# New orders of steps, new signals and new PSUM banks for a gated cross-attention and expert kernel in fp32

## The reference: what is computed

```python
x = x + tanh(g_xattn) * xattn(layernorm(x), ctx, ctx)
x = x + tanh(g_ffn) * ffn(layernorm(x))
```

```python
gate = softmax(h2 @ Wg + bg)
combined = einsum('btd,edf,bte->btf', h2, We, gate)
```

## Time and profile before

| what | value |
|---|---|
| median of 3 runs | 1069.57 us (1068.63 to 1070.08) |
| the profiled execution's own time | 1069.42 us |
| its span | 1067.6 us |
| busy: TensorE, its weight loads | 1012.6 (95%), 831.4 (78%) |
| busy: DVE, ScalarE, GpSimd | 961.4 (90%), 758.7 (71%), 752.5 (70%) |
| chain that ended last | TensorE 87%, DVE 5%, GpSimd 4% |

### The profile page before, as it was taken

One profiled execution on the slowest core, in us unless ns is written; L12 is line 12 of the kernel. 1 busy time (PEld: TensorE's weight loads), 2 busy tenths in 40 slices (PEclk: granted clock), 3 DMA queues, 4 the chain that ended last, 5 costly groups with the idle time before them and its releaser, 6 DMA issues.

```text
span 1067.6 us, 32201 instructions
## 1 busy us (share of the span) xinstructions
PE 1012.6 (95%) x12870; PEld 831.4 (78%) x12870; DVE 961.4 (90%) x2176; ACT 758.7 (71%) x1564; POOL 752.5 (70%) x1111
## 2 busy tenths in 40 slices
PE   1568999999999999999999999999999999999998
PEld 0447788788888888888888888888888888888787
DVE  7778888999999999999999999999999999998996
ACT  6678877776677777668777666877766687776541
POOL 4578877787677778767778766777876677787531
PEclk9989999999999999999999999999999999999999
DMA  9501000011000001100100100010111000000000
GB/s 311 169 21 31 12 24 29 31 31 31 23 28 25 22 31 31 32 21 24 29 22 32 32 31 22 21 32 21 32 32 31 22 22 31 22 21 12 12 11 30
DMA packets 38915, 38.67 MB, mean 36 GB/s; under 512 B 3440, under 2 KB 38512, under 8 KB 38768
## 3 DMA queue, kind: packets, MB, share of 16 engines
q1 hardware_dynamic: 38384, 36.59, 10.9%
q0 software_dynamic: 384, 0.04, 0.0%
HBM read 28.23 MB, written 8.39 MB: 34 GB/s over the span
## 4 chain that ended last, share of the span: by engine, by line
PE 87%; DVE 5%; POOL 4%; issue 1%; ACT 1%; DMA 0%; SPq 0%; POOLq 0%; DVEq 0%; ACTq 0%
PE ps L2302 15%; PE ps L2304 14%; PE ps L2303 14%; PE ps L2333 10%; PE ps L2348 9%; PE ps L2341 5%; PE ps L2317 5%; PE ps L2382 3%; PE ps L2373 3%; PE ps L2296 2%; PE ps L2358 2%; DVE hk L1770 2%; PE ps L2366 1%; PE ps L2367 1%; PE ps L2325 1%
## 5 line engine op out<-in xcount | busy, mean ns | idle before, releaser
L1434 DVE SCALAR_TENSOR_TENSOR z<-ps,gate,z 128x256 f32<-128x256 f32 x512 | 238.5, 472 | 37.9 <-PE ps L2304 29.0
L2302 PE MATMUL ps<-we_hi,h_hi 128*128 128x512 f32 (+2 forms) x640 | 240.5, 376 | 0.6 <-DVE z L1434 0.4
L2304 PE MATMUL ps<-we_hi,h_lo 128*128 128x512 f32 (+2 forms) x640 | 224.1, 350 | 0.0
L2303 PE MATMUL ps<-we_lo,h_hi 128*128 128x512 f32 (+2 forms) x640 | 223.7, 349 | 0.0
L2302 PEld LDWEIGHTS ps<-we_hi,h_hi 128*128 128x128 f32 x640 | 120.4, 188 | 36.7 <-issue 12.6
L2333 PE MATMUL ps<-qf,kf 64*128 64x256 f32 x1024 | 129.2, 391 | 9.1 <-POOL kf L549 4.5
L2304 PEld LDWEIGHTS ps<-we_hi,h_lo 128*128 128x128 f32 x640 | 120.2, 188 | 17.1
L2303 PEld LDWEIGHTS ps<-we_lo,h_hi 128*128 128x128 f32 x640 | 120.8, 189 | 11.5
L2333 PEld LDWEIGHTS ps<-qf,kf 64*128 64x128 f32 x1024 | 96.4, 191 | 29.8 <-issue 11.3
L2348 PE MATMUL ps<-att,v 128*32 128x256 f32 (+1 forms) x2048 | 109.0, 329 | 3.1 <-POOL att L540 0.9
L911 ACT ACTIVATE att<-ps 128x512 f32<-128x512 f32 x32 | 19.1, 597 | 116.8 <-PE ps L2333 116.7
(11 more groups left out here) (232 smaller groups left out, 3079.7 us busy)
## 6 DMA issues: line engine op xcount, KB each, us to landing
x_in<-in_x SPq DMA_DIRECT2D x32, 256.0 KB, 2.6
c_in<-in_ctx SPq DMA_DIRECT2D x32, 256.0 KB, 2.6
out<-z SPq DMA_DIRECT2D x32, 256.0 KB, 2.2
c_chunk<-in_ctx SPq DMA_DIRECT2D x14, 512.0 KB, 8.0
stage<-in_L_ffn_We SPq DMA_DIRECT2D x2, 1024.0 KB, 10.0
c_chunk<-in_ctx SPq DMA_DIRECT2D x2, 256.0 KB, 6.5
stage_b<-in_L_ffn_bup SPq DMA_DIRECT2D x1, 256.0 KB, 6.9
stage_q<-in_L_ffn_Wq SPq DMA_DIRECT2D x1, 256.0 KB, 6.4
```

The lines of the kernel that those rows point to most:

```text
L1434: return dve.scalar_tensor_tensor(out=z[b % 2][:, t, :], in0=ps[:, bank, offset:offset + D], scalar=gate[:, t, ex:ex + 1], in1=z[b % 2][:, ...
L2302: pe.matmul(out, a_hi(c), b_hi(c), start=(c == 0), stop=False)
L2303: pe.matmul(out, a_hi(c), b_lo(c), start=False, stop=False)
L2304: last = pe.matmul(out, a_lo(c), b_hi(c), start=False, stop=(c == C - 1))
```

## The change

Nothing is computed in another way. On all five engines the first slots, the steady slot and the last steps are listed in a new order; the steady loop starts at n = 5 in place of 6. The waits follow the new order, the signals are grouped anew (13 semaphores for TensorE's steps in the loop, 12 before), and 43 of the 48 entries of `BANK` are new. TensorE's slot, as the lists read (`+1` stands for batch n + 1):

```diff
-h2_t1(-3) h2_t0(-3) mm13(-4) dn(-1) fq(+1) mm1g(-3) mm0g(-3) o_tr(-2) mm12(-3) kv0(-1) kv1(-1) o(-2)
-mm10(-3) mm11(-3) X00(+1) X01(+1) Y0(+1) Y1(+1) X11(+1) X10(+1) av0(+1) s(-1) av1(+1)
-mm00(-3) mm01(-3) hn_t(0) mm02(-3) fkp(+2) av2(+1) pv(-1) av3(+1) fk(+2) mm03(-3) nt_t(+1) qq(0)
+o(-2) mm0g(-3) mm1g(-3) dn(-1) fq(+1) mm00(-3) mm11(-3) mm10(-3) kv1(-1) kv0(-1) mm01(-3)
+X01(+1) X00(+1) Y0(+1) X11(+1) X10(+1) Y1(+1) av0(+1) s(-1) av1(+1) hn_t(0)
+mm12(-3) mm13(-3) mm02(-3) mm03(-3) av2(+1) pv(-1) av3(+1) fkp(+2) fk(+2) nt_t(+1)
+o_tr(-1) h2_t0(-2) h2_t1(-2) qq(0)
```

GpSimd's slot:

```diff
-pq0(+1) pk0(+1) d_v(-1) pq2(+1) pq3(+1) v1(+1) pq1(+1) z0(-2) x1(0) v_bd(-1) m01(+1) m00(+1) k_lo(+2)
-g_r(0) yb(-1) m10(+1) q_r(+2) r2(-2) m11(+1) pk2(+2) q_lo(+2) pk1(+2) o_n(-1) pk3(+2)
+pk1(+1) q_lo(+1) z0(-2) x1(0) pk2(+1) pq2(+1) pq0(+1) d_v(-1) pq1(+1) pk0(+1) pk3(+1) pq3(+1) g_r(0)
+r2(-2) m00(+1) k_lo(+2) m01(+1) q_r(+2) m10(+1) v_bd(-1) m11(+1) yb(-1) o_n(-1) v1(+2)
```

The part of the diff with the banks and with the waits of the steps that the prediction speaks of:

```diff
-BANK = dict(stab=0, fk0=6, fk1=4, fk2=3, fk3=7, fq0=0, fq1=2, fq2=4, fq3=1, x000=3, x001=1, x010=0, x011=5,
-            y00=3, y01=7, av0=3, x100=0, x101=2, x110=5, x111=4, y10=1, y11=6, av1=2, nd0=2, nd1=0, ht=1,
+BANK = dict(stab=2, fk0=2, fk1=3, fk2=5, fk3=4, fq0=6, fq1=7, fq2=2, fq3=0, x000=6, x001=4, x010=1, x011=7,
+            y00=2, y01=1, av0=2, x100=3, x101=0, x110=7, x111=5, y10=4, y11=6, av1=7, nd0=1, nd1=0, ht=3,
...
+            def X01_(b):
+                if b >= 4:
+                    pe.wait_ge(*at("a00", b - 4))
+                if b >= 2:
+                    pe.wait_ge(*at("bqq", b - 2))
...
+                pe.wait_ge(*at("pq3", b))
+                first_keys(b, 0, 1, BANK["x010"], BANK["x011"]).then_inc(*up("X01", b))
...
             def Y0_(b):
...
+                pe.wait_ge(*at("x010", b))
+                second_keys(b, 0, BANK["y00"], BANK["y01"]).then_inc(*up("Y0", b))
```

More of the change, by code:

```diff
@@ L386, in _ @@
             load_x_(6)
-            store_(1)
-            load_x_(7)
-            load_c_(8)
-            for n in range(6, NB + -1):
+            for n in range(5, NB + -1):
                 slot(n)
@@ new lines, in g_r_ @@
+            @per_batch
+            def g_r_(b):
+                pool.wait_ge(*at("g_bn", b))
+                if b >= 1:
+                    pool.wait_ge(*at("y", b - 1))
+                for which in range(2):
+                    pool.tensor_scalar(shift_f[:, which, :], mvg[:, :, 0], -1.0, 1.0, ALU.mult, ALU.mult)
+                pool.tensor_tensor(r_f[:, :, :].rearrange("p a b -> p (a b)"), var_f[:, :, :].rearrange("p a b -> p (a b)"),
+                                   neg_half[:, 0:2 * T], ALU.pow).then_inc(*up("r_f", b))
+                pool.wait_ge(*at("r_f", b))
+                pool.tensor_tensor(shift_f[:, :, :], shift_f[:, :, :], r_f[:, :, :], ALU.mult).then_inc(*up("g_r", b))
@@ L1994, in _ @@
+            h_lo_(1)
+            h_tr_(1)
+            wo_hi_()
+            q_bn_(1)
+            y00_(0)
+            h_lo_(2)
+            y01_(0)
+            x_t_(1)
+            y10_(0)
+            we_lo2_()
+            y11_(0)
+            c_t_(2)
+            b_kv_()
+            wo_lo_()
+            wdn_hi_()
+            we_lo3_()
             h_tr_(2)
-            wo_hi_()
+            off_tok_()
+            wq_hi_()
             den_(0)
             o_x_(0)
-            wq_hi_()
+            we_lo1_()
@@ L2492, in o_, with mm00_ @@
-            @per_batch
-            def o_(b):
-                if not b:
-                    pe.wait_ge(*at("bqq", b + 1))
-                if b >= 4 and b + 3 < NB:
-                    pe.wait_ge(*at("eq3", b + 3))
-                pe.wait_ge(*at("ot_lo", b))
-                for t in range(T):
-                    last = three_passes(ps[:, BANK["o"], t * D:(t + 1) * D], tok(ot_hi, t), tok(ot_lo, t), cols(wo_hi, 0, D), cols(wo_lo, 0, D))
-                last.then_inc(*up("o", b))
+            def mm00_(b):
+                if b >= 1:
+                    pe.wait_ge(*at("a02", b - 1))
+                expert_products(b, 0, slice(0 * D, 2 * D), BANK["mm00"]).then_inc(*up("mm00", b))
@@ L2841, in _ @@
             av3_(3)
+            fkp_(4)
+            fk_(4)
+            nt_t_(3)
+            o_tr_(1)
             h2_t0_(0)
```

2528 lines of the change are left out of this document (1175 added, 1353 removed).

## The result

The changed kernel took 1070.95 us in the median of 20 runs (1068.81 to 1073.35), the kernel before 1069.59 in the median of 20. The ratio is 1.0016, with a 95% interval from 1.0009 to 1.0022: slower by 1.4 us, less than the 0.2% that I had named as what one comparison can tell, but with twenty runs each clear of no change. Forecast were 1061.6, between 1056.5 and 1067.2. The prediction was wrong in its sign and outside its range.

What follows compares the result with a forecast made beforehand. TensorE was taken as the bound, busy 199.89 of 200 us in steady state. Terms: 25 slots at -.18 (-4.5), first slots -3.0, last slots -.4, together -7.9 us, giving 1061.6 us, range 1056.5 to 1067.2.

Steps and rivals of the forecast that it cites:

- Item 1: Keys' feature products grouped on TensorE, three changes of array form for four: -.34 us a slot, bounds -.39 and -.20.
- Item 2: Score products and mask: Y halves apart, 0 (bounds 0, +.10); GpSimd's mask issued earlier, -.09 us a slot.
- Item 3: First score product newly waits for GpSimd's fourth query feature, chain 10.04 against TensorE's 9.86: +.18 us, bounds 0 and +.40.
- rival C: GpSimd sets the slot, its eleven steps each stretching: at 60 ns each +.34 us a slot, 1078 us; chance .04.
- Item 4: Attention output transposed in its own slot, waiting for GpSimd's normalization: +.10 us a slot, bounds 0 and +.40.
- The head scores: Head scores on TensorE no longer wait for the second Y: -.03 us a slot.
- Items 6 and 7: First slots: shorter stop before batch 1's score product and less low clock, -3.0 us; last slots, reordered work, -.4 us.
- TensorE's 33 us from 40 to 80: Sign for the start: TensorE busy about 33 us between 40 and 80 us, where it was 30.01.
- a stop under 3 us: Sign for the start: the 4.1 us stop of a score product waiting for a query feature falls under 3.
- A: Rival: the new waits don't come, since DVE's sum starts earlier; -.36 us a slot, 1057 us; chance .20.
- D: Rival: banks or late signals cost, not array form, so grouping gives nothing; +.16 us a slot, 1070 us; chance .03.
- B: Rival: wait for the fourth query feature +.30 to +.40, nothing gained at the start; 1067.5 to 1070 us; chance .06.

Runs made afterwards that it cites:

- bz: The kernel before, with GpSimd's two residual steps moved behind the slot's second mask and a third buffer for the tile they read: 1084.59 us, 1.0138.
- gz: bz with the keys' norm round also moved forward to their three feature rounds, ahead of the third attention step: 1080.42 us, 1.0102 to the kernel before.
- z1: The changed kernel, with GpSimd's two residual steps moved behind the slot's second mask and a third buffer for their tile: 1059.21 us, 0.9903 to the kernel before.
- bz2: The kernel before, with GpSimd's residual steps moved further back, behind q_r where GpSimd is idle: 1087.17 us, 1.0170.

## Why the prediction was wrong, point by point

- *Item 1, grouping*: forecast -.34. The rows give .75 - .43 = -.32, and bz with gz shows .17 for leaving out one change of form in the kernel before. Right in mechanism, shown there by the pair; the size in the changed kernel stands on its rows. The figures for a change held within .03 in a place where they had not been seen.
- *Item 2, mask and Y*: the mask, -.09, right. For Y I took 0 with a bound of +.10; it cost +.08, because the wait that comes last in time had become the separate one of two. A mis-sized term: the bound was right and the value not.
- *Item 3, the wait for the fourth query feature*: the step that failed, a term of the sum that was too small. Forecast +.18, measured .34 at the score products and .09 at the keys-values products, .43. The chain took 10.33, not 10.04: .13 more from the residual steps to the first feature (the gap behind a long addition, 1.38 from start to start where the row that I read had another neighbour, 1.26), .06 in the feature steps and the cast, .09 in the signal, .01 in DVE's start. TensorE's side, .34 and .09 taken off, is 9.90 (z1, where nothing waits, has 9.87), and I had 9.86. Nearly all the error is in the chain, by .29, and rival C, which I gave .04, asked for .32. It was the right mechanism with a far too small chance: a margin of .18 between two sums of ten microseconds is less than what the gaps between eleven instructions can hide. The .02 to .03 per step that I had called unlikely was there. Over 25 slots the .25 are 6.3 of the 9.3 us between forecast and result.
- *Item 4, the normalized output*: +.10 forecast, +.05 measured (.49 for the transposes in place of .44).
- Not seen at all: the transposes `hn_t` behind `av1` have a cheaper change than the experts that stood there, -.06.
- The head scores: -.03, as forecast (.67 behind the attention step for .70). But the reason was another: bz has the same .67 with the Y products still together and only the mask's wait gone.
- Sum per slot: -.32 - .09 + .08 + .43 + .05 - .06 - .03 = +.06, as the means of the slots have it, and 25 x .06 = +1.5. I had -.18 and -4.5.
- *Items 6 and 7*: forecast -3.4. The spans differ by +1.2, so start and end gave 1.2 - 1.5 = -.3, which is the other 3.1 us of the miss. The 2 us at the first score product came, and more, and the clock's stretch behind it was halved (3.4 us for 6.8), more than the third that I had taken; what I took as 0 (batches 2 to 4 in their new order) took both back, with the second stretch at the lower clock behind DVE's three stops. Two of my signs failed with it: TensorE's 33 us from 40 to 80, and a stop under 3 us, which is 3.83. I had read one stop of the first slots and not asked which would be the next, which is late for DVE. No run takes these stops away, so this part is read from the traces and not shown.
- *The rivals*: A (the waits don't come) needed the sum of DVE to begin earlier; it began at .22, as assumed. D falls with item 1. B and C together are what happened: item 3 at .43 and nothing at the start, which is B a little beyond its upper end, by C's chain.
- The Trainium skill's rule in the page TensorEngine Tiling (Array Packing), Tiling Modes, Key Properties (a change of tiling mode drains TensorE) agrees with .09 to .18 for each change here. The Trainium skill's rule in the GPSIMD Engine Reference, Key points, on the SBUF interfaces shared with VectorE, names VectorE's instructions with two SBUF inputs or in a 2-port mode. It shows in this kernel in other places than the feature steps of the earlier trace rows that I had read: `gb`, which has two such inputs, took .95 us beside a long addition and .18 with GpSimd idle. `var_f` has one, and no row shows its mode.

## What to carry to other kernels

When a new order brings a wait within a few tenths of a microsecond of a chain on another engine, the stretch between the chain's start and that wait lasts as long as the longer of two sums. Gains of the shorter side inside the stretch are worth nothing; gains outside it, as the grouping here, still count. Measure the chain from start to start, gaps included, and give the case that it is late its full chance. Before work is regrouped on the busy engine, ask which engine's queue the other side of the loop runs through, and take from that queue first what nobody waits for (here two residual steps and one buffer, 11.7 us). A dummy instruction in the suspected place and the same one in an idle place (here +.55 us a slot and 0) tell in two runs whether a chain sets the time.

## What the runs showed of the hardware

- Some DVE instructions of a few columns that work in SBUF do not end before the GpSimd instruction that was running when they began: `var_f` took 1.17 us for a median of .31 in bz2; in the changed kernel the gate's `gb` has a median of .95 us beside the residual steps, before .37, in z1, where they lie elsewhere, .38. The short times are held as well: in 29 or more of the 32 slots the end falls .02 to .04 us behind the end of GpSimd's instruction, a mask, a cast or a feature step of .62 in the short ones, and the few `gb` with GpSimd idle take .17 to .18.
- The other way round as well: a feature step of GpSimd of .62 us took 1.57 in the first slots of the changed kernel beside a DVE instruction on two tiles of 128x1024, which ran from 57.37 to 58.65:

```profile
57.56 1.57 POOL L447 TENSOR_SCALAR qf<-qf 128x512 f32<-128x512 f32 x1
```

- Of two waits ahead of a TensorE instruction the one written second became an instruction of its own ahead of the weight load (in the changed kernel's trace at 513.92, for the copy that ended at 513.88); where it is also the last in time, the products start .14 behind the event in place of .05.
- GpSimd's copies and casts start .05 to .06 us before the printed end of an addition of 1.28 us, feature steps .08 behind it (medians of the slots).
